# Loading the first matrices of experts 5 to 7 earlier, and splitting expert 2's weights during the shared down projections

## The reference, cut to what matters

```python
xt = layernorm(x).reshape(T, d)                        # T = 1024, d = 256
probs = softmax(xt @ Wg); eidx = argmax(probs)         # 8 experts
keep = pos < C                                         # C = 128 rows for each expert
xd = zeros(E * C, d).at[flat].set(xt, mode='drop')     # rows sorted by expert
h  = silu(xd[e] @ W1[e]) * (xd[e] @ W3[e])             # W1, W3: 256 x 352
oe = h @ W2[e]                                         # W2: 352 x 256
out = oe[flat] * gate
shared = (silu(xt @ sw1) * (xt @ sw3)) @ sw2
return x + out + shared
```

## Time and profile before

| | before |
|---|---|
| median of 3 runs | 167.0 us (166.19 to 167.06) |
| the profiled execution: its own time | 165.67 us |
| the profiled execution: its span, first to last instruction | 163.9 us |
| PE busy | 147.9 us, 90% of the span |
| DVE, ACT, POOL busy | 101.9, 86.8, 65.1 us |
| mean granted TensorE clock | 0.992 of full speed |
| moved by the DMA engines | 18.43 MB, 112 GB/s on average |
| transfer size: W1 or W3 of one expert | 352 KB |
| transfer size: W2 of one expert, in two pieces | 256 KB and 96 KB |
| transfer size: one store of `out` | 128 KB |

### The profile page before, as it was taken

One profiled execution on the slowest core, in us unless ns is written; L12 is line 12 of the kernel. 1 busy time (PEld: TensorE's weight loads), 2 busy tenths in 40 slices (PEclk: granted clock), 3 DMA queues, 4 the chain that ended last, 5 costly groups with the idle time before them and its releaser, 6 DMA issues.

```text
span 163.9 us, 3537 instructions
## 1 busy us (share of the span) xinstructions
PE 147.9 (90%) x1291; PEld 102.8 (63%) x1291; DVE 101.9 (62%) x250; ACT 86.8 (53%) x201; POOL 65.1 (40%) x88
## 2 busy tenths in 40 slices
PE   7697998998899999999999998999899799969940
PEld 2344544554455555555546687997899799859830
DVE  0399864779778787876141546679764875667220
ACT  3443256673856565674767197347533964375300
POOL 7124818502904533150202000075894278227350
PEclk9999999999999999999999999999999999999996
DMA  3990351725080700000260000011339949932110
GB/s 93 352 351 25 96 174 26 246 69 199 8 262 4 253 7 6 0 6 0 48 218 6 2 0 0 6 65 65 111 82 317 293 84 342 337 105 88 64 58 32
DMA packets 15697, 18.43 MB, mean 112 GB/s; under 512 B 1852, under 2 KB 14949, under 8 KB 15680
## 3 DMA queue, kind: packets, MB, share of 16 engines
q1 hardware_dynamic: 14240, 14.98, 28.7%
q0 software_dynamic: 1152, 2.97, 5.5%
q10 hardware_dynamic: 288, 0.26, 0.6%
HBM read 14.12 MB, written 4.21 MB: 112 GB/s over the span
## 4 chain that ended last, share of the span: by engine, by line
PE 70%; DVE 8%; ACT 6%; DMA 6%; issue 4%; POOL 3%; SPq 0%; ACTq 0%; POOLq 0%; DVEq 0%
PE bank L969 15%; PE bank L1006 10%; PE bank L990 9%; PE bank L1202 5%; PE bank L1143 4%; PE bank L1178 4%; PE bank L1179 4%; DMA wraw<-in_w 3%; PE bank L923 3%; PE bank L1056 3%; PE bank L1058 3%; DMA xs<-in_x 2%; PE bank L1018 2%; PE bank L1033 2%; DVE nm L518 2%
## 5 line engine op out<-in xcount | busy, mean ns | idle before, releaser
L518 DVE TENSOR_REDUCE nm<-bank 128x2 f32<-128x512 f32 x64 | 40.9, 684 | 12.6 <-PE bank L969 12.6
L769 ACT ACTIVATE pt<-bank 128x512 f32<-128x512 f32 x64 | 34.5, 589 | 15.3 <-PE bank L990 15.1
L990 PE MATMUL bank<-qz,kz 32*128 32x256 f32 x256 | 41.3, 403 | 0.8 <-ACT pt L769 0.8
L969 PE MATMUL bank<-kz,qz 32*128 32x256 f32 x256 | 35.8, 404 | 1.4 <-DVE qz L496 1.4
L969 PEld LDWEIGHTS bank<-kz,qz 32*128 32x128 f32 x256 | 21.6, 184 | 12.4 <-issue 6.4
L990 PEld LDWEIGHTS bank<-qz,kz 32*128 32x128 f32 x256 | 24.9, 184 | 6.4 <-ACT pt L769 4.3
L1006 PE MATMUL bank<-pt,vext 128*32 128x256 f32 x256 | 20.2, 391 | 0.0
L431 POOL DMA_INDIRECT expert_rows<-rk,idx_s x8 | 8.0, 1002 | 22.8 <-DVE rk L606 21.0
L367 POOL TENSOR_SCALAR qz<-xs,rs,mrs 128x256 f32<-128x256 f32 x14 | 7.7, 561 | 23.1 <-DVE mrs L490 23.1
L1202 PE MATMUL bank<-wraw,kz 128*128 128x256 f32 (+1 forms) x48 | 11.8, 384 | 1.6 <-DVE rlo L663 1.3
L465 POOL DMA_INDIRECT out<-vext,rk x8 | 7.9, 988 | 11.6 <-DMA vext<-out,rk 5.9
(11 more groups left out here) (146 smaller groups left out, 317.8 us busy)
## 6 DMA issues: line engine op xcount, KB each, us to landing
wraw<-in_w SPq DMA_DIRECT2D x16, 352.0 KB, 3.8
wraw<-in_w SPq DMA_DIRECT2D x8, 256.0 KB, 3.8
expert_rows<-zero SPq DMA_DIRECT2D x1, 1032.0 KB, 5.2
out<-xs SPq DMA_DIRECT2D x8, 128.0 KB, 3.4
xs<-in_x SPq DMA_DIRECT2D x3, 256.0 KB, 4.8
cs<-in_ctx SPq DMA_DIRECT2D x3, 256.0 KB, 5.0
wraw<-in_w SPq DMA_DIRECT2D x8, 96.0 KB, 3.9
wraw<-in_sw SPq DMA_DIRECT2D x2, 352.0 KB, 5.6
```

What stands on the lines that cost most here:

```text
L518: nc.vector.tensor_reduce(nm[:, b % 2, :, place], scores_bank[:].rearrange("p (u c) -> p u c", u=2), AX_X, ALU.max, negate=True).then_inc( ...
L769: nc.scalar.activation(pt[:, g % NPT, n % 4, :], sc_bank[n % NS][:], ACT.Exp).then_inc(exped, 1)
L969: mm = nc.tensor.matmul(scores_bank[:, u * D:(u + 1) * D], qz[rows, b, half, u * P:(u + 1) * P], kz[rows, b, half, :], start=True, stop=True)
L990: mm = nc.tensor.matmul(sc_bank[n % NS][:, c * D:(c + 1) * D], kz[rows, b, half, c * P:(c + 1) * P], qz[rows, b, half, :], start=True, sto ...
```

## The change

The load of an expert is cut into `load_expert_up` (W1 and W3, counted on `ld_w`) and `load_expert_down` (W2, counted on a new semaphore `ld_w2`). `expert_high` now waits for the first two transfers only, and `expert_down` on PE waits for the other two. SP issues the up load of expert 5 between the sixth and the seventh store of `out`, those of 6 and 7 right behind the eighth store, and then the three down loads with their waits. Apart from that, `expert_high(2, ·)` on ACT moves into the shared stage and `expert_low(2, ·)` on DVE to a place ahead of `expert_hidden(0)`.

```diff
-            def load_expert(e):
+            def load_expert_up(e):
                 n = e % NW
...
+            def load_expert_down(e):
+                n = e % NW
+                t = wts[n]
                 if e >= NW:
                     sp.wait_ge(e_down, e - NW + 1)
                 sp.dma_start(t[:, W2:W2 + 2 * D].rearrange("p (c d) -> p c d", c=2),
-                             w2[e, 0:2 * P].rearrange("(c p) d -> p c d", p=P)).then_inc(ld_w[n], 16)
-                sp.dma_start(t[0:FL, W2 + 2 * D:WCOLS], w2[e, 2 * P:F]).then_inc(ld_w[n], 16)
+                             w2[e, 0:2 * P].rearrange("(c p) d -> p c d", p=P)).then_inc(ld_w2[n], 16)
+                sp.dma_start(t[0:FL, W2 + 2 * D:WCOLS], w2[e, 2 * P:F]).then_inc(ld_w2[n], 16)
...
             for b in range(B):
                 sp.wait_ge(shared_added, b + 1)
                 sp.dma_start(out[b], xs[:, b, :]).then_inc(base_stored, 16)
+                if b == B - 3:
+                    load_expert_up(NW)
+            for e in range(NW + 1, E):
+                load_expert_up(e)
             for e in range(NW, E):
-                load_expert(e)
+                load_expert_down(e)
...
             rows_low(1)
+            expert_low(2, 0)
+            expert_low(2, 1)
             for e in range(E):
                 expert_hidden(e)
                 if e >= 2:
                     expert_out(e - 2)
                 if e + 2 < E:
                     rows_low(e + 2)
-                    expert_low(e + 2, 0)
-                    expert_low(e + 2, 1)
+                    if e >= 1:
+                        expert_low(e + 2, 0)
+                        expert_low(e + 2, 1)
...
-                act.wait_ge(ld_w[e % NW], 16 * 4 * ring_pass(e, NW))
+                act.wait_ge(ld_w[e % NW], 16 * 2 * ring_pass(e, NW))
...
-                if b < 5:
+                if b < 7:
                     expert_high((b - 1) // 2, (b - 1) % 2)
...
-                if e + 2 < E:
+                if 1 <= e < E - 2:
                     expert_high(e + 2, 0)
...
                     expert_rows(e + 2)
-                    expert_high(e + 2, 1)
+                    if e >= 1:
+                        expert_high(e + 2, 1)
...
                 pe.wait_ge(eh_copied, e + 1)
+                pe.wait_ge(ld_w2[e % NW], 16 * 2 * ring_pass(e, NW))
```

More of the change, by code:

```diff
@@ L244, in block_kernel @@
         ld_w = [sem(f"ld_w{i}") for i in range(NW)]
+        ld_w2 = [sem(f"ld_w2{i}") for i in range(NW)]
         ld_m = [sem(f"ld_m{i}") for i in range(2)]
@@ L313, in load_expert @@
                 sp.dma_start(t[:, W2:W2 + 2 * D].rearrange("p (c d) -> p c d", c=2),
-                             w2[e, 0:2 * P].rearrange("(c p) d -> p c d", p=P)).then_inc(ld_w[n], 16)
-                sp.dma_start(t[0:FL, W2 + 2 * D:WCOLS], w2[e, 2 * P:F]).then_inc(ld_w[n], 16)
+                             w2[e, 0:2 * P].rearrange("(c p) d -> p c d", p=P)).then_inc(ld_w2[n], 16)
+                sp.dma_start(t[0:FL, W2 + 2 * D:WCOLS], w2[e, 2 * P:F]).then_inc(ld_w2[n], 16)
+            def load_expert(e):
+                load_expert_up(e)
+                load_expert_down(e)
             sp.dma_start(leni[:], bass.AP(tensor=lens.tensor, offset=lens.offset,
```

## The result

The changed kernel takes 169.38 us as the median of 4 runs (169.00 to 170.76); the kernel before took 166.68 beside it (166.19 to 167.06, 4 runs). The ratio is 1.018, with a 95% interval of 1.012 to 1.024 (a ratio is taken from those executions of a kernel that lie within 1.5% of its fastest one): the change makes the kernel slower by some 3 us. The forecast was 166.8, the range 164.5 to 169.0.

What follows compares the result with a forecast made beforehand. It took the last quarter's chain of waits, mostly PE work, as the bound: 3.03 us saved by parts 1 and 2, eaten by a 2.8 us stop at down(1), leaving -0.2 and a forecast of 166.8 us, range 164.5 to 169.0.

Steps and rivals of the forecast that it cites:

- rival B: First gather fares like the later ones, taking 6.0 us; down(1) starts after 138.4; shift +1.6, 168.6 us; chance 0.27.
- Part 1: Expert 2's halves made earlier: up(2) on PE follows its transposes at once, at 128.73 instead of 129.89, -1.16 us.
- Part 2: First matrices loaded apart: the waits for late weights of experts 5 and 6 go, -0.37 and -1.50 us.
- Part 3: Last two stores behind 704 KB of loads: last store 2.2 us later, bounds +1.0 and +2.7; first gather starts at 132.1.
- The gather's length: First gather beside the loads of experts 6 and 7: 4.2 us instead of 2.8, landing at 136.3; ends 2.8 and 6.5.
- Rival A: First gather hardly waits and stays near its quiet 2.8 us; shift between -2.9 and -1.0, put at -2.2, 164.8 us; chance 0.28.
- What waits for it: expert_out(0), rows_low(4) and down(1) wait for the first gather; down(1) starts 1.0 us after its landing, or at 134.51 if later.
- The length of the pause and its price: PE stands 2.8 us at down(1), eating the 3.0 saved; a clock drop was allowed for only at B's upper end.
- The sum: Whole kernel shifts by -0.2 us, to a span of 163.7 us for the profiled execution.

Runs made afterwards that it cites:

- first_gather: Changed kernel with all eight stores first, then expert 5's up load, and those of 6 and 7 only after the first gather landed: 163.46 us, ratio 0.986 to before.
- after: The changed kernel itself, against the kernel before: 169.38 us, ratio 1.018; its profiled execution took 170.76 us.
- after_again: The changed kernel measured once more without edits, beside the kernel before: 169.20 us, ratio 1.021.
- hold_67: Changed kernel, but SP issues the up loads of experts 6 and 7 only when all eight stores have landed: 170.76 us, one execution.
- loads_only: Changed kernel with expert 2's halves put back to their old places, loads as in the change: 168.36 us, ratio 1.010 to before.
- stores_first: Changed kernel with expert 5's up load moved behind the eighth store, with those of 6 and 7: 165.92 us, ratio 0.995 to before.
- w1_between: Changed kernel with only W1 of expert 5 (352 KB) between the sixth and seventh store, W3 behind the eighth: 167.96 us, ratio 1.001 to before.
- busy_pe: Changed kernel with 70 small unused matmuls on PE between up(3) and down(1), in place of the pause: 167.23 us, ratio 1.008 to before.
- before_again: The kernel before, profiled a second time without edits: 165.75 us in one execution.
- swap_out: Changed kernel with rows_low(e+2) ahead of expert_out(e-2) on DVE: 167.38 us, ratio 1.010 to before.

## Why the prediction was wrong

The prediction said no change, and the kernel is slower. The measured 169.38 us lies above the range, and down(1) starts after 138.4 us in both profiles of the changed kernel (139.79 and 138.92), which the prediction had named as its sign for rival B. B's time was near, 168.6 us, but not for B's reason, a gather of 6.0 us. Two steps failed: how late the last store lands, and what a pause of PE costs.

- Part 1, right. up(2) starts 0.14 behind its transposes and nothing else is held up. Part 2, right. ACT's roundings wait for no transfer and the turns are 3.76. The sum of both, 3.03, was found in first_gather as 2.86 against the profile that the prediction was read from, and as 1.97 against the second one of before.
- Part 3, the last store: mis-sized. I gave it +2.2 within +1.0 and +2.7. From up(0) the gather starts 3.76 later after, and 2.66 in after_again. The upper bound was no bound: I took the moment at which the old kernel's W3 landed, 131.7, as that at which the queue is free. There both loads stood behind the stores and came last. Behind 704 KB the store lands 1.8 to 2.7 us later than the some 3.0 without (2.7 to 3.3, then 4.8 to 5.7), and its issue is a further 1.0 late. That makes 2.8 to 3.7. I read it so that the store's own way of some 3.0 us starts only when the bytes ahead have passed; at 0.39 MB in a microsecond, as below, 704 KB take 1.9 us, which gives an estimate of 4.9. Why some executions lie up to 0.8 above that isn't shown. In after the queue moved little just then. For 129 to 130 us the view of the queues has:

```profile
q1 hardware_dynamic: 157, 0.21, 95.3%
```

  and for 134 to 135, with the loads of experts 6 and 7 and no store:

```profile
q1 hardware_dynamic: 295, 0.39, 105.8%
```

  But that is not the cause of the spread: the same microsecond has 0.24 MB in after_again and 0.29 in hold_67, whose stores took 4.8 and 5.5 us.
- The gather's length: the number was near, 4.4 and 4.5 in the two profiles of the changed kernel for the 4.2 taken, but in part by luck. The prediction added a length to a start. In the other kernels with loads on the way the length went from 3.6 (loads_only) to 5.8 (stores_first), as the landing followed the end of the loads. Two readings beside it were a little off: six of the eight gathers of before took clearly longer than 2.8 us (3.7 to 6.5), not four or five, and A's shift begins at -2.8 by its own G, not at -2.9.
- Rival A didn't come. It leaned on a gather near its quiet length. But the gather took 2.9 us without the loads and up to 5.8 with them, and in stores_first its queue moved nothing for the first 3.9 us. The Trainium skill, page "DMA: Bandwidth & Descriptors", section "Queues, rings and completion order", says that each engine goes round-robin between the queue rows, a packet at a time. The conclusion that the prediction drew from it, a gather that hardly waits, doesn't hold here; whether the engines take turns, these views can't tell.
- What waits for it, right. From the gather's landing to down(1) it is 1.0 us (138.80 to 139.79). down(1) came at up(0) + 14.86, where the prediction had 13.18: 1.53 from the store, 0.2 from the gather.
- The length of the pause and its price: the second failed step. The prediction held PE's stop of 2.8 us to cost only itself, and kept a fall of the clock for the upper end of rival B. The clock fell with pauses of 4.95 (hold_67), 4.11 (after), 3.19 (after_again), 2.75 (w1_between) and 1.89 us (stores_first), and stayed at 1.2 GHz for some 3 to 7 us, most of it with work on PE. In the profiled execution that is 24.31 - 21.53 = 2.78 us, busy_pe being the same stage at full clock. The prediction's own stretch from down(1) to the last scatter was 34.71 - 13.18 = 21.53: all of its turns were right but for the clock.
- The sum, on the profiled execution: 0.8 us from ahead of up(0), which before_again shows too; then -0.2 as predicted, +1.68 by the late down(1), +2.78 by the clock. That is 5.1, against 5.0 of span. That execution was the slowest of its four. In after_again, which took 168.64 us, the gather started only 0.43 later than predicted, down(1) 0.75 later, and the stretch behind it took 23.06, 1.53 more than predicted: there the clock was two thirds of the miss. On the medians, where it is +2.7, about 1.4 are left with the clock held, and the rest is the clock.

What stays open is why the same last store landed after 4.8 us in two kernels' profiles and after 5.5 to 5.7 in four others, and when exactly the clock falls: a pause of 1.93 (swap_out) left it alone, one of 1.89 (stores_first) did not. Single executions of before had a clock of 0.980 to 0.982 too, 4 of 25, and took 168.4 to 169.5 us; they were not profiled, so where theirs fell isn't known.

## What to carry to other kernels

A small transfer that something waits for goes ahead of bulk loads in its queue, and the loads that nobody needs yet wait until that small transfer's reader, here the first gather, has landed: first_gather gains 1.4% by that from a change that lost 1.8%. To price a transfer put behind others, add the time of the bytes ahead to its full quiet latency, and don't read the end from a trace in which those bytes came last. A saving ahead of a wait with a fixed end only lengthens the wait, and on TensorE a longer wait can cost its clock. Here that came after five pauses of 1.89 to 4.95 us, and not after one of 1.93 or those under 1.3: so price a pause of this length with what comes behind it, 1.5 to 2.8 us in the two profiles of the changed kernel.

## What the runs showed of the hardware

- Loads that run beside an indirect gather make it up to twice as long: 2.9 us quiet (first_gather), 3.6 in loads_only, 4.4 and 4.5 in after and after_again, 5.3 in hold_67, 5.8 in stores_first, although the loads lie in another queue. In stores_first the gathers' queue moved no packet from the issue at 130.80 to 134.75, while the loads moved 0.39 MB in a microsecond.
- Replacing a pause by 70 matmuls whose result nobody reads made the kernel faster: the ratio to before is 1.008 (1.006 to 1.011) in place of 1.018 (1.012 to 1.024). The clock went through the same stretch at 1.00.
- The same program at a clock of 0.990 and of 0.979 differs by some 2.4 us (w1_between: 165.5 to 166.2, and 167.4 to 168.8). The profile with the pause of 2.75 us is one of the second group; that the others' pauses were shorter is possible and wasn't seen.
